# Graph layer and expert layer on one core: the 0/1 matrix of destinations and the edge weights are put in PSUM

## The reference

```python
# graph layer, h = layernorm(x)
h_fwd, h_rev = h @ W_forward.T, h @ W_reverse.T                  # 6250 x 64 each
messages = h_fwd[src] * w[:, 0:1] + h_rev[src] * w[:, 1:2]       # one row per edge
scores = leaky_relu(messages @ attn.T, 0.2)                      # 4 heads
e = exp(scores - scores.max(axis=0))
norm = e / (segment_sum(e, dst)[dst] + 1e-10)
out = segment_sum(messages * norm[:, head], dst)                 # for each of 4 heads
x = x + out.reshape(6250, 256)
# expert layer: top 2 of 16 experts, FFN 256-512-256, added, layernorm, added to x
```

## Time and profile before

| | us |
|---|---|
| median of 3 runs | 2537.11 |
| lowest and highest | 2532.44, 2537.75 |
| the profiled execution, its own time | 2544.06 |
| span of its trace, first to last instruction | 2542.3 |
| first to last gather of the edge stage | 61.97 to 1881.35 |
| busy in the span: PE, DVE, ACT, POOL | 2020.8, 1854.4, 349.5, 1709.5 |

### The profile page before, as it was taken

One profiled execution on the slowest core, in us unless ns is written; L12 is line 12 of the kernel. 1 busy time (PEld: TensorE's weight loads), 2 busy tenths in 40 slices (PEclk: granted clock), 3 DMA queues, 4 the chain that ended last, 5 costly groups with the idle time before them and its releaser, 6 DMA issues.

```text
span 2542.3 us, 44100 instructions
## 1 busy us (share of the span) xinstructions
PE 2020.8 (79%) x11977; PEld 1765.1 (69%) x11978; DVE 1854.4 (73%) x4481; ACT 349.5 (14%) x936; POOL 1709.5 (67%) x1757
## 2 busy tenths in 40 slices
PE   7688888887888888788888888888727579999970
PEld 6577777676777777667777777777626568888870
DVE  6777777877777787777778777777747866666657
ACT  4100000000000000000000000000015524444435
POOL 6777777777777777777777777777745753333327
PEclk9699999999999899999999999999955589999995
DMA  6222222222222222222222222222244676655657
GB/s 203 61 63 59 64 59 64 61 59 63 59 64 58 63 61 59 63 59 64 58 64 61 59 64 59 64 58 64 57 135 131 211 228 199 196 196 197 198 167 270
DMA packets 176304, 256.65 MB, mean 101 GB/s; under 512 B 47078, under 2 KB 120999, under 8 KB 176004
## 3 DMA queue, kind: packets, MB, share of 16 engines
q0 software_dynamic: 53696, 121.60, 19.5%
q1 hardware_dynamic: 122564, 134.56, 17.3%
HBM read 218.11 MB, written 38.79 MB: 101 GB/s over the span
## 4 chain that ended last, share of the span: by engine, by line
POOL 42%; issue 25%; DVE 15%; PE 6%; DVEq 5%; DMA 5%; ACT 1%; SPq 0%; POOLq 0%; ACTq 0%
POOL rows L262 42%; DVEq L1704 3%; DMA rows<-node_table,index 2%; PE p_y L1872 1%; DVE p_y L1927 1%; PE p_h L1862 1%; DVE shared L985 1%; PE p_win L878 1%; DVE second L1907 1%; DVE hid_t L1899 1%; DVE p_part L994 1%; DVE back L1912 1%; DMA out<-shared 1%; DVE msg L1023 1%; DMA shared<-in_x 1%
## 5 line engine op out<-in xcount | busy, mean ns | idle before, releaser
L262 POOL DMA_INDIRECT rows<-node_table,index x1375 | 1378.3, 1002 | 443.8 <-issue 423.7
L966 PE MATMUL p_hot<-parts,onehot 128*128 128x476 f32 x5264 | 1193.4, 387 | 9.4 <-DVE rows L1059 5.1
L966 PEld LDWEIGHTS p_hot<-parts,onehot 128*128 128x128 f32 x5264 | 1003.7, 192 | 169.7 <-issue 14.4
L878 PE MATMUL p_win<-hot_ex,msg 128*65 128x64 f32 x3136 | 282.3, 268 | 334.4 <-DVE hot_ex L1027 333.3
L878 PEld LDWEIGHTS p_win<-hot_ex,msg 128*65 128x65 f32 x3136 | 267.5, 182 | 372.4 <-issue 372.4
L990 DVE TENSOR_TENSOR rows<-rows,index 128x1088 f32<-128x1088 f32 x98 | 126.7, 1292 | 333.0 <-DMA rows<-node_table,index 332.0
L1713 POOL DMA_INDIRECT expert_rows<-ys,back x104 | 103.0, 990 | 270.9 <-DVE ys L1932 199.0
L928 ACT ACTIVATE ex<-score,neg_shift 128x64 f32<-128x64 f32 x98 | 34.2, 349 | 1758.0 <-DVE score L1011 1758.0
L1054 DVE SCALAR_TENSOR_TENSOR p_hot<-place_no,place_of_source,p_hot 128x476 f32<-128x476 f32 x376 | 249.9, 709 | 0.0
L985 DVE TENSOR_TENSOR shared<-shared,p_win 65x64 f32 x784 | 170.3, 217 | 97.0 <-PE p_win L878 4.0
L1059 DVE TENSOR_REDUCE rows<-p_hot 128x136 f32<-128x952 f32 x188 | 216.1, 1150 | 6.5
(11 more groups left out here) (268 smaller groups left out, 1408.2 us busy)
## 6 DMA issues: line engine op xcount, KB each, us to landing
shared<-in_w SPq DMA_DIRECT2D x120, 512.0 KB, 4.5
rows<-node_table,index POOLq DMA_INDIRECT x1375, 2.8
xs<-dispatched SPq DMA_DIRECT2D x104, 129.5 KB, 4.1
key<-hot_keys SPq DMA_DIRECT2D x94, 128.0 KB, 3.0
shared<-expert_rows SPq DMA_DIRECT2D x12, 896.0 KB, 7.8
token_rows<-in_x SPq DMA_DIRECT2D x7, 896.0 KB, 13.1
shared<-in_x SPq DMA_DIRECT2D x7, 768.0 KB, 9.0
out<-shared SPq DMA_DIRECT2D x6, 896.0 KB, 7.5
```

The source lines that it names most:

```text
L262: pool.indirect_dma_start(out=rows[:, s, k, :], out_offset=None, in_=table, in_offset=bass.IndirectOffsetOnAxis(ap=index[:, s, 0, k:k + 1] ...
L878: last = pe.matmul(psum[0:MSG, u * HEADS * W:(u + 1) * HEADS * W], msg[:, k, :], weighted[:, k, :, :].rearrange("p h w -> p (h w)"), start ...
L966: last = pe.matmul(p_hot[:, j, d, 0:PLACES * COLS], onehot[:, j, gr, :], parts[:, gr:NT:GP, m, d * COLS:(d + 1) * COLS], start=(gr == 0 an ...
```

## The change

`hot` is no longer an SBUF tensor of bf16. It becomes 256 fp32 columns of `p_dve`. Another 32 columns of `p_dve`, `weight_p`, receive a copy of the chunk's two edge weights, made by VectorE with a new instruction ahead of `all_rows`, which waits for `index`. L990, L994 and L997 read the weights from there, L1027 reads `hot` there. SyncE now reloads `index` once the copy is made (`weights_copied`), where it waited for `rev_score`.

```diff
-            hot = sb("hot", [P, K, W], BF16)
@@
+            hot_at = W + K * HEADS + GP
+            weight_at = hot_at + K * W
+            assert weight_at + 2 * K <= 512 - HEADS * W
+            weight_p = p_dve[:, weight_at:weight_at + 2 * K].rearrange("p (d k) -> p d k", d=2)
+            hot = p_dve[:, hot_at:hot_at + K * W].rearrange("p (k w) -> p k w", k=K)
@@
+            weights_copied = sem("edge_weights_in_psum")
@@ SyncE
-                    sp.wait_ge(rev_score, c - RING + 1)
+                    sp.wait_ge(weights_copied, c - RING + 1)
@@ VectorE
                 def step(c, s, it, loaded):
+                    dve.wait_ge(index_ready[s], 16 * (it + 1))
+                    after(dve, raw_ready, c)
+                    after(dve, rev_part, c)
+                    dve.tensor_copy(weight_p, index[:, s, 1:3, :].bitcast(F32)).then_inc(weights_copied, 1)
                     all_rows(dve, c, s, it)
-                    attr_of = index[:, s, 1:3, :].bitcast(F32)
+                    dve.wait_ge(weights_copied, c + 1)
+                    attr_of = weight_p
```

## The result

| | before | after |
|---|---|---|
| median of 4 runs each, us | 2535.86 | 2461.03 |
| lowest and highest | 2532.44, 2537.75 | 2460.88, 2461.21 |
| ratio, 95% interval | | 0.9706 [0.969, 0.9723] |
| last gather ends, in the trace | 1881.35 | 1802.0 |
| gathers of L262, busy in all | 1378.3 | 1300.9 |

The kernel is 2.9% faster. The forecast was 2461 us. Lines after the edit move by 4 to 10; L1000, L1004, L1007, L1037 are the old L990, L994, L997, L1027, L1033 is the old L1023, L1026 the old L1016, L1069 the old L1059, and L996 is the new copy.

A forecast was written before the change was run, and what follows sets the result against it. GpSimd's gathers were taken to bound the edge stage. 2544.06 − 78.3 for stalls + 2 left over gave 2467.8 us for the profiled execution; less its 6.95 us over the median, 2461 us, range 2449 to 2481.

The forecast's parts named there:

- The bound: Edge stage: GpSimd issues gather after gather at a pitch of 1.25 us, while VectorE and TensorE wait in every chunk.
- The stalls, 78.3 us: Gathers held by L990, L994, L997 and L1027, which read two SBUF operands; 78.3 us go if all four stop blocking.
- the three long gathers ahead of the loop: Set-up: long gathers, together 0.6 us over the median, the longest 1.21 us, that stay.
- Left over, 2 us: L1011 and L1016 still read two SBUF operands; 0.02 us a chunk lost, 2 us in all, at worst 22.
- rival A: Gathers meet L1011 and L1016 in every chunk; gain smaller by 10 to 22 us, time 2469 to 2481, chance 0.12.
- The total: Whole kernel: 2467.8 us for the profiled execution, 2461 us as the median.
- The 6.95 us taken off at the end: Whole kernel: the profiled execution before lay 6.95 us above the median of 2537.11, so this was subtracted.
- The copy, 0: Weights' copy ahead of `all_rows`: 0.2 us a chunk, hidden in VectorE's wait for rows; costs nothing, bounds 0 to 20 us.
- The changed operands, −0.1 to +0.5 us a chunk, taken as 0: L990, L994, L997, L1027 reading PSUM and L1003 writing it: no slower, none of it on the path.
- The room behind it: Slack per chunk after the change: VectorE from 3.26 to about 2.4 us, TensorE from 3.03 to about 2.2.
- Rivals C and D: C: VectorE becomes the bound, 2595 us, chance 0.02; D: TensorE sets the pace, about 2490 us, chance 0.03.

The follow-up runs named there:

- e6_fill_1: The changed kernel plus an idle VectorE copy of 1024 columns, SBUF to PSUM, about 1.15 us, at each chunk's end; 2460.73 us.
- e1: The kernel before with only `hot` moved to PSUM, edge weights still read from SBUF; 2478.83 us against 2539.81, ratio 0.9753.
- e2: The changed kernel with `hot` back in SBUF as bf16, so only the weights are in PSUM; 2530.73 us, ratio 0.996 to before.
- e4: The changed kernel with `p_part` in SBUF as bf16, so the sum making `msg` reads two SBUF inputs; 2540.33 us, ratio 1.0006 to before.
- e5: The kernel before with `hot` as fp32 in place of bf16, still in SBUF; 2539.3 us, ratio 0.9999.
- e8: Two kernels: the one before plus an idle VectorE reduction ahead of L1023, of 640 or 384 columns; 2497.04 and 2572.71 us against 2540.69.
- e3_copy_unused: The kernel before plus the weights' copy into PSUM and a wait for it ahead of L990, the copy never read; 2549.3 us, ratio 1.0032.
- e7: The kernel before plus the unused copy of the weights, without the added wait ahead of L990; 2541.61 us against 2540.11, ratio 1.0001.
- e6_fill_3: The changed kernel plus an idle VectorE reduction of 3072 columns, about 3.35 us, at each chunk's end; 2547.32 us, ratio 1.0029 to before.
- e8_shift_048: The kernel before plus an idle VectorE reduction of 384 columns, about 0.48 us, ahead of L1023; 2572.71 us, ratio 1.0126.

## Why the prediction was right

*The bound.* GpSimd set the edge stage before and sets it after: the gaps between the gathers are 443.8 and 443.6 us, and what left their busy time left the run. The chain of the page after gives VectorE 28% and GpSimd 22%, which could be read as a change of bound. `e6_fill_1` shows that it is none: its chain gives VectorE 29% and GpSimd 19%, and 1.15 us a chunk more for VectorE cost nothing. Why the chain leans to VectorE was not tried.

*The stalls, 78.3 us.* 77.4 went. The cause stood as argued: two inputs in SBUF (`e1`, `e2`, `e4`), whatever the type of `hot` (`e5`). The moment decides, as said, though its bounds are narrower at the start of an instruction than the theory had them (`e8`). The Trainium skill's page "SBUF — State Buffer", section "Who interferes with whom", has both rules that the prediction weighed. The runs agree with the one that two SBUF inputs contend with a GpSimd instruction that reads SBUF, here at up to 1.13 us a gather. The remark there that `tensor_tensor` doesn't stall GpSimd's DMAs, whose reason is marked as inferred, doesn't hold for these gathers, which read their node numbers from SBUF.

Two inputs are enough, but they are not the only thing that holds a gather. One of the three long gathers ahead of the loop stands beside L735, a CAST with one SBUF input and its output in SBUF. In the trace of `e3_copy_unused` they meet more fully:

```profile
75.52 0.56 DVE L735 CAST firsts<-lohi 1x784 int32<-1x784 f32 x1
75.57 1.33 POOL L262 DMA_INDIRECT rows<-node_table,index  x1 [0.30 <-issue]
```

This gather, too, ends 0.82 us after the instruction. The copy of 1024 columns from SBUF into PSUM in `e6_fill_1` held none of the 95 gathers that met it. Which other instructions of VectorE hold a gather was not tried; in the loop no gather lost over 0.03 us without a two-input one beside it. The prediction counted the three as stalls that stay, which they did (1.20, 1.04, 1.20 us); the first of them, ahead of which GpSimd had been idle, has no such instruction beside it and is not explained.

*Left over, 2 us.* It did not come: L1016 was to miss its gather by 0.05 us, and no gather is held by it. It ends at 1009.67 in the chunk above; the gather starts at 1009.68. Read at 0.13 us, that is a miss by 0.14. The chunk from which the 0.05 was taken was a late one: its L990 starts 2.77 us after the last gather, where the median is 2.68. Over the whole trace after the miss is 0.11 us in the median and 0.01 at the least. So rival A failed by about a tenth of a microsecond of phase, which is luck; the lines that could have made it true are still there. The gathers that lose nothing ran 2 ns longer in the median in this one trace (945 to 947, 2.8 us in all); in `e6_fill_1` they took 944, so this is no effect of the change.

*The total.* The mechanism is shown; that the median fell on the forecast to the microsecond is partly luck. The sum had 2467.8 us for a profiled execution, and it took 2461.21. In the terms of the sum 0.7 us less went than forecast (77.6 with the gaps, for 78.3), the 2 left over were not lost, and 5.2 lie in front of and behind the gathers, where the profiled execution of before had been long. The 6.95 us taken off at the end happened to cover these. Against the later medians of before the gain is 79 us, not 75.

*The copy, 0.* Right for this kernel, and less simply than argued. The prediction named VectorE's slack as the cover, which holds (`e7`). It said of the added wait only that it is met by then. `e3` shows that a met wait still starts L990 0.09 us later, and that this costs 0.3% as long as a gather is held until L990's end. In the changed kernel no gather is, so nothing is left of it.

*The changed operands, −0.1 to +0.5 us a chunk, taken as 0.* The three long products are 1 to 4 ns shorter, L1013 11 ns longer.

*The room behind it.* 2.4 and 2.2 us a chunk were forecast for VectorE and TensorE; 2.41 and 211.9 / 85 = 2.49 were measured. The 2.4 is 3.26 − 0.8 and left out the copy, which at its 0.2 us would have made it 2.3. The copy fills only 0.11 us of the wait (L1054 ends at 1003.87, the copy at 1003.98), and the added wait, which counts as waiting, gives most of that back. The prediction also took the wait for `msg` for GpSimd's tightest, with 4.7 us of slack. That for the scores was tighter: in its chunk they are ready at 1016.73,

```profile
1016.51 0.22 DVE L1011 SCALAR_TENSOR_TENSOR score<-raw 128x64 f32<-128x64 f32 x1
```

and gather 7, which waits for them, starts at 1020.87, 4.1 us later. `e6_fill_3` bears that out: it is for the scores that GpSimd waits there. Nothing in the forecast hung on it. Rivals C and D never came near.

*The count by halves.* The prediction did not give one. My expectation for the weights alone, 19 us, took a total of stalls as a sum of independent ones and was twice what came.

## What to carry to other kernels

When GpSimd issues indirect DMAs without a pause, look at the shortest, the mean and the longest of them: a spread over equal work suggests a stall, and the engine that is inside an instruction when the long ones start is the suspect. Then compare instructions that hold it with ones of the same length that don't, operand by operand; here one operand in PSUM decided. Until such stalls are gone, an edit to VectorE's order can move the time by its phase alone: here a wait that was always met cost 0.3%, and two pieces of idle work gained 1.8% and lost 1.3%.

## What the runs showed of the hardware

- A gather that meets an instruction of VectorE with two SBUF inputs is held until that instruction ends, and then needs another 0.80 to 0.83 us, where a free one takes 0.94. It meets it if the instruction still runs about 0.13 us after the gather's start and did not begin later than 0.04 to 0.07 us after it (L1034 in `e8_shift_048`).
- It is held by one instruction only. The gather at 1014.43 ends 0.82 us after L990, while L994, also with two SBUF inputs, has been running since 0.08 us before L990's end.
- A CAST with one SBUF input, within SBUF, held a gather too (1.33 us, `e3_copy_unused`); a copy from SBUF to PSUM did not (`e6_fill_1`, 95 gathers).
- It does not work the other way: L990 took 1291 to 1314 ns in all 98 chunks of the kernel before, also where a gather had started first.
- A wait on VectorE that was already met cost 0.09 us ahead of the instruction behind it (`e3` against the kernel before, 2.77 and 2.68 us after the last gather; 2.67 without it in `e7`).
- An instruction of VectorE with one operand in PSUM was no slower than with both in SBUF: 1214 against 1215 ns for 1024 columns.
- GpSimd pauses 2.1 us every 112 gathers, before and after. What it does there was not tried; the 12 pauses are some 22 us of the changed kernel (12 times 2.1 less the usual 0.3).
